# Input rows of the feed-forward part transposed on VectorE instead of TensorE, in a gated cross-attention block on one core

## The reference

```python
x = x + tanh(g_xattn) * xattn(layernorm(x), ctx)          # x: 2 x 2048 x 512, fp32
x = x + tanh(g_ffn)   * ffn(layernorm(x))
# ffn, w_gate and w_up (1536 x 512) and w_down (512 x 1536) int32, scaled by 1/127:
#   silu(x @ w_gate.T) * (x @ w_up.T) @ w_down.T
# xattn: 16 heads of 32, 77 context rows per batch, softmax over them, causal mask, output projection
```

## Time and profile before

| | |
|---|---|
| median of 3 runs | 874.59 us (873.66 to 875.28) |
| the profiled execution's own time | 874.07 us |
| its span, first to last instruction | 872.3 us |
| TensorE busy | 855.0 us (98%) |
| VectorE busy | 652.8 us (75%) |
| ScalarE busy | 460.5 us (53%) |
| GpSimd busy | 402.3 us (46%) |
| granted TensorE clock | 1.000 of full speed |
| FFN, four pairs | from 372.55 us to the end |

### The profile page before, as it was taken

How to read it: one execution, slowest core, us unless ns; L and a number is a source line. 1 busy time by engine, 2 the same in 40 slices (tenths; PEclk the granted TensorE clock), 3 DMA queues, 4 the chain that set the end, 5 groups by cost and what they waited for, 6 DMA issues and landing times.

```text
span 872.3 us, 12869 instructions
## 1 busy us (share of the span) xinstructions
PE 855.0 (98%) x4087; PEld 707.9 (81%) x4087; DVE 652.8 (75%) x1081; ACT 460.5 (53%) x1130; POOL 402.3 (46%) x344
## 2 busy tenths in 40 slices
PE   8999999999999999999999999999999999999997
PEld 7678888888888887788888888888888888888876
DVE  5988877778786877679688478788487877587882
ACT  5687575666666757446056264165362364460550
POOL 4665555556564664437144444155253255251350
PEclk9999999999999999999999999999999999999999
DMA  9233847272728131567333256043265143243302
GB/s 334 73 109 118 276 152 248 84 240 93 233 97 277 68 113 51 198 235 265 115 123 133 96 190 249 12 165 121 79 248 182 47 164 113 96 166 116 97 31 98
DMA packets 60406, 128.73 MB, mean 148 GB/s; under 512 B 7616, under 2 KB 20416, under 8 KB 60352
## 3 DMA queue, kind: packets, MB, share of 16 engines
q1 hardware_dynamic: 58960, 125.95, 41.7%
q10 hardware_dynamic: 1392, 2.10, 0.7%
HBM read 99.93 MB, written 27.79 MB: 146 GB/s over the span
## 4 chain that ended last, share of the span: by engine, by line
PE 87%; DVE 6%; ACT 3%; issue 1%; DMA 1%; POOL 1%; ACTq 0%; DVEq 0%
PE psum L1814 34%; PE psum L1548 29%; PE psum L1864 18%; PE psum L1573 4%; DMA gates<-g_ffn 1%; PE psum L1657 1%; ACT e L791 1%; POOL hT L696 1%; DVE bn L1034 1%; DVE e L1076 1%; DVE K L1128 1%; DVE mx L1073 1%; DVE qT L1058 0%; DVE pT L1047 0%; DVE aT L1058 0%
## 5 line engine op out<-in xcount | busy, mean ns | idle before, releaser
L1814 PE MATMUL psum<-xv,ring 128*128 128x512 f32 x1344 | 308.2, 390 | 0.9 <-ACT a L964 0.7
L1814 PEld LDWEIGHTS psum<-xv,ring 128*128 128x128 f32 x1344 | 251.5, 188 | 55.1 <-ACT a L964 1.1
L696 POOL TENSOR_TENSOR hT<-th,hT 128x512 fp32r<-128x512 f32 x48 | 86.3, 1798 | 201.2 <-ACT hT L984 201.2
L1864 PE MATMUL psum<-w_d,hT 128*128 128x512 f32 x768 | 177.7, 391 | 1.3 <-POOL hT L696 0.8
L1864 PEld LDWEIGHTS psum<-w_d,hT 128*128 128x128 f32 x768 | 143.7, 188 | 32.6 <-POOL hT L696 2.0
L554 POOL TENSOR_TENSOR e<-e,rden 128x616 f32<-128x616 f32 x64 | 77.9, 1217 | 110.4 <-DVE rden L1110 73.8
L791 ACT ACTIVATE e<-psum,nmx,q_scale 128x77 f32<-128x77 f32 x256 | 102.6, 427 | 2.3 <-DVE nmx L1090 2.2
L952 ACT ACTIVATE a<-psum 128x512 f32<-128x512 f32 x48 | 28.7, 599 | 131.7 <-PE psum L1814 131.4
L1428 DVE SCALAR_TENSOR_TENSOR acc<-psum,gate_ffn,acc 128x512 f32<-128x512 f32 x64 | 47.7, 750 | 65.1 <-PE psum L1864 65.1
L1548 PE MATMUL psum<-wo,aT 128*128 128x512 f32 x384 | 95.2, 399 | 0.5 <-DVE aT L1058 0.5
L1548 PE MATMUL psum<-xT,wq 128*128 128x512 f32 x360 | 89.0, 398 | 0.4 <-DVE qT L1058 0.4
(11 more groups left out here) (110 smaller groups left out, 1204.6 us busy)
## 6 DMA issues: line engine op xcount, KB each, us to landing
ring<-w_var SPq DMA_DIRECT2D x48, 896.0 KB, 4.6
w_var<-stage SPq DMA_DIRECT2D x12, 896.0 KB, 4.6
x_ln<-x SPq DMA_DIRECT2D x32, 256.0 KB, 4.6
x_res<-x SPq DMA_DIRECT2D x32, 256.0 KB, 5.0
x_mid<-x_res SPq DMA_DIRECT2D x32, 256.0 KB, 2.0
x<-x_mid SPq DMA_DIRECT2D x16, 512.0 KB, 5.6
acc<-x_mid SPq DMA_DIRECT2D x16, 512.0 KB, 6.4
out<-acc SPq DMA_DIRECT2D x32, 256.0 KB, 2.0
```

The costliest lines, as they stand in the source:

```text
L696: nc.gpsimd.tensor_tensor(hT[:, 1, i % HH, j, :], h[:, :], hT[:, 0, i % HH, j, :].bitcast(f32), ALU.subtract).then_inc(h_lo, 1)
L1814: last = nc.tensor.matmul(psum[:, bank, :], stat, mov, start=start and j == 0, stop=j == len(terms) - 1, skip_group_check=not start)
L1864: last = nc.tensor.matmul(m_bank[t % 2][:, :], hT[:, a, m, t // TT, (t % TT) * P:(t % TT + 1) * P], w_d[:, HH * h + m, :], start=m == 0 an ...
```

## The change

For pairs 1 to 3 (pair 0 stays as it is):

- The 32 TensorE transposes per pair are replaced by 32 VectorE transposes per pair, each of 32 partitions by 512 elements (`turn_rows`). They write `x2_t0` and `x2_t1` in SBUF. They are put at the end of slices 5 and 6 (two each), between the results of the first half's down tiles (two or three after each, 20 in all), and at the end of slices 7, 8 and 9 (three, three, two).
- The statistics move to slices 1 to 4. The normalisation moves from VectorE to GpSimd, in slices 3 and 4, after `h_low`.
- The load of the next pair's rows is issued at the start of the pair, all four DMAs in a row; for pair 1 before the last stores of attention.
- SiLU is one activation on ScalarE; both multiplies on VectorE go. The constant in `gate_ffn` follows.
- T1 and T3 are formed in slices 10 and 11 on VectorE, from SBUF, and written over the rows in `x2`, which are dead by then. T2 and T4 follow after slice 11. GpSimd's low part of T1 comes before its `h_low` of slice 11.
- The maximum over the gate and up weights is taken in all slices of the last pair, no longer in the first six of pair 0.
- At the end of a pair TensorE's order is rewritten: three down tiles are begun instead of two, the third in a bank of the slices, and their first slots are put before, between and behind p4 and p3.

```diff
+            def turn_rows(q, half_of, ops):
+                tiles = slice(TT * half_of, TT * half_of + TT)
+                dve.wait_ge(x2_normed, PT * q + TT * (half_of + 1))
+                if q > 1:
+                    dve.wait_ge(xb_lo, nth(XB_ORDER, q - 1, B22))
+                for op in ops:
+                    a, c = divmod(op, HG)
+                    rows = x2[a * HD:(a + 1) * HD, tiles, :].rearrange("p t (k n) -> p t k n", n=P)
+                    to = x2_t[half_of][c * HD:(c + 1) * HD].rearrange("p k (t n) -> p t k n", n=P)
+                    nc.vector.transpose(to[:, :, :, a * HD:(a + 1) * HD], rows[:, :, :, c * HD:(c + 1) * HD])\
+                        .then_inc(x2_turned, 1)
...
-                nc.scalar.activation(th1[:, :], psum[:, set_a[i % 2], :], ACT.Tanh, scale=0.5 * W_SCALE)\
-                    .then_inc(tanh1_done, 1)
+                nc.scalar.activation(th1[:, :], psum[:, set_a[i % 2], :], ACT.Silu, scale=W_SCALE)\
+                    .then_inc(silu1_done, 1)
...
                 if more:
-                    xv_copy(p + 1, B11, b11_at)
-                tanh2(last)
-                tanh1(last)
+                    xv_round(p + 1, B11)
+                silu2(last)
+                silu1(last)
                 if more:
-                    b12_copy(p + 1)
+                    xv_high(p + 1, T1)
                 h_high(last, 0)
+                if more:
+                    xv_round(p + 1, B21)
                 h_high(last, 1)
                 if more:
-                    xv_high(p + 1, T1)
-                    xv_copy(p + 1, B21, b21_at)
                     xv_high(p + 1, T2)
                     xv_high(p + 1, T3)
                     xv_high(p + 1, T4)
-                    b22_copy(p + 1)
+                    xv_round(p + 1, B22)
...
             def pair(p):
+                if 0 < p < NP - 1:
+                    sp.wait_ge(xv_lo, nth(LO_ORDER, p, T4))
+                    for j in range(TT):
+                        load_x2(p + 1, j)
                 for m in range(MH):
...
-                    if p + 1 < NP and m < TT:
-                        sp.wait_ge(xb_full, nth(TURNED, p, B21))
-                        load_x2(p + 1, m)
...
# GpSimd, in slice m behind h_low
-                    if p + 1 < NP and m == HH - 1:
-                        rstd_ahead(2 * p + 2)
-                        rstd_ahead(2 * p + 3)
+                    if p + 1 < NP and m in (2, 4):
+                        rstd_ahead(2 * p + 1 + m // 2)
+                        mean_ahead(2 * p + 1 + m // 2)
+                    if p + 1 < NP and m in (3, 4):
+                        normalise(2 * p - 1 + m)
+                    if p + 1 < NP and m == MH - 2:
+                        xv_low(p + 1, T1, T1)
...
# VectorE
+            FILL = (4, 6, 8, 11, 13, 16, 18, 21, 24)
             def first_half(p, more):
                 for t in range(PT):
-                    if more:
-                        stats2(2 * p + 2 + t // TT, t % TT)
...
                     result(p, 0, t)
-                    if more and t >= PT - 2:
-                        normalise2(2 * p + 2, range(2 * (t - PT + 2), 2 * (t - PT + 2) + 2))
-                if more:
-                    normalise2(2 * p + 3)
+                    if more:
+                        turns(p + 1, range(FILL[t], FILL[t + 1]))
...
# TensorE, end of a pair
-                if more:
-                    turn(p + 1, B11)
-                    turn(p + 1, B12)
+                early, late = range(HH - 2), range(HH - 2, HH - 1)
+                down(p, 1, 0, early)
                 p4(last)
+                down(p, 1, 1, early)
                 p3(last)
-                down(p, 1, 0, range(HH - 1))
-                down(p, 1, 1, range(HH - 1))
+                down(p, 1, 2, early)
+                for t in range(3):
+                    down(p, 1, t, late)
...
-                down(p, 1, 0, range(HH - 1, HH))
-                down(p, 1, 1, range(HH - 1, HH))
-                if more:
-                    turn(p + 1, B22)
-                    turn(p + 1, B21)
-                for t in range(2, PT):
+                for t in range(3):
+                    down(p, 1, t, range(HH - 1, HH))
+                for t in range(3, PT):
                     down(p, 1, t)
```

More of the change, by code:

```diff
@@ L1250, in form @@
+            def form(q, j):
+                if q:
+                    dve.wait_ge(x2_turned, turned(1, q))
+                else:
+                    if j == T1:
+                        dve.wait_ge(b12_kept, 1)
+                    dve.wait_ge(xb_full, nth(TURNED, 0, {T1: B11, T2: B22, T3: B22, T4: B21}[j]))
+                if j == T2:
+                    dve.wait_ge(v_formed, formed(q, T1))
+                if j == T4:
+                    dve.wait_ge(v_formed, formed(q, T2))
                 if j == T1:
-                    dve.wait_ge(b12_kept, q + 1)
@@ L1266, in xv_low @@
+                nc.vector.tensor_tensor(variant(q, j), one, other, ALU.subtract).then_inc(v_formed, 1)
             def xv_low(q, j, bank):
                 dve.wait_ge(xv_hi, nth(HI_ORDER, q, j))
-                nc.vector.tensor_tensor(xv[:, j, 1], pair_of(bank), xv[:, j, 0].bitcast(f32), ALU.subtract)\
+                full = {B11: b11, B21: b21, B22: b22}[j] if q else pair_of(bank)
+                nc.vector.tensor_tensor(xv[:, j, 1], full, xv[:, j, 0].bitcast(f32), ALU.subtract)\
                     .then_inc(xb_lo, 1)
@@ L1449, in widest, with turns @@
                 nc.vector.tensor_copy(wide[:, :], wide_f[:, :]).then_inc(wide_ready, 1)
+            def turns(q, ops):
+                for half_of in range(2):
+                    inside = [op - TURNS * half_of for op in ops if op // TURNS == half_of]
+                    if inside:
+                        turn_rows(q, half_of, inside)
+            FILL = (4, 6, 8, 11, 13, 16, 18, 21, 24)
             def first_half(p, more):
                 for t in range(PT):
-                    if more:
-                        stats2(2 * p + 2 + t // TT, t % TT)
-                    elif t < HH:
+                    if not more and t < HH:
                         dve.wait_ge(rd_used, HH)
@@ L1478, in pair @@
                         hidden2(i - 1)
-                    if p == 0 and m < HH or p == NP - 1 and m >= HH:
+                    if p == NP - 1:
                         largest_gu(i)
+                    if more and 1 <= m <= TT:
+                        for t in (2 * m - 2, 2 * m - 1):
+                            stats2(2 * p + 2 + t // TT, t % TT)
+                    if more and m in (HH - 1, HH):
+                        turns(p + 1, range(2 * (m - HH + 1), 2 * (m - HH + 2)))
+                    if more and HH < m < HH + 4:
+                        at = (24, 27, 30, 32)[m - HH - 1:m - HH + 1]
+                        turns(p + 1, range(at[0], at[1]))
+                    if more and m == MH - 2:
+                        form(p + 1, T1)
+                    if more and m == MH - 1:
+                        form(p + 1, T3)
                 gate2(last)
-                silu2(last)
                 if more:
                     xv_low(p + 1, B11, b11_at)
-                silu1(last)
                 hidden1(last)
@@ L1488, in pair @@
                 hidden2(last)
-                if not more:
+                if more:
+                    form(p + 1, T2)
+                else:
                     widest()
-                if more:
-                    form(p + 1, T1)
                 result(p, 1, 0)
                 result(p, 1, 1)
-                if more:
-                    form(p + 1, T2)
-                    form(p + 1, T3)
                 result(p, 1, 2)
@@ L1500, in pair @@
                     xv_low(p + 1, B21, b21_at)
-                    form(p + 1, T4)
                 result(p, 1, 3)
                 if more:
+                    form(p + 1, T4)
+                result(p, 1, 4)
+                if more:
                     xv_low(p + 1, B22, b22_at)
-                for t in range(4, PT):
+                for t in range(5, PT):
                     result(p, 1, t)
```

225 lines of the change are left out of this document (104 added, 121 removed).

## The result

The change made the kernel slightly slower. It takes 875.65 us (median of 12 runs, 875.37 to 877.38) against 873.88 for the kernel before (12 runs, 873.13 to 875.28): a ratio of 1.0021, interval 1.0013 to 1.003. The forecast was 866.5. The profiled execution took 875.89 us with a span of 874.0, and 874.07 with 872.3 before.

What follows compares the result with a forecast made beforehand. TensorE, busy 98% of the span, was taken to bound the kernel. Gains of 6.9 us (2.3 at each of three pairs' ends) and 1.2 (last pair) sum to 8.1, giving 866.5 us against the median; range 864 to 869.5, chance 0.65.

Steps and rivals of the forecast that it cites:

- the term 0.228 us a matmul: TensorE: time per matmul, read from 72 matmuls at a pair's end and used throughout the sum.
- nothing: GpSimd, slices 3 and 4: loads of 6.2 and 7.6 us against 6.4 cost TensorE no time; pair 0 up to half a microsecond.
- VectorE's transposes: VectorE: 0.68 us each, 22 us a pair for 32, covered by removed work; no cost to TensorE in the slices.
- The rival of a slow transpose: VectorE transposes at 1.21 us each stall TensorE 5.7 us a pair, 17 in all, giving 883.5 us; chance 0.08.
- SiLU: ScalarE: one extra table load before the first SiLU, `snap2` 0.25 us later, no cost; by the skill's figure 0.6 us worse.
- The rival of a load in each slice: ScalarE reloads its table at every change between SiLU and Copy: 53 us over 44 slices, near 920 us; chance 0.03.
- The end of a pair: TensorE at a pair's end: 3.9 us removed less 1.6 of new stalls, gaining 2.3 a pair, 6.9 for three.
- the zero of the forecast: At a pair's end: the point at which TensorE has issued p7 of slice 11, from which the steps are timed.
- the stall of 0.6: At a pair's end: TensorE waits for GpSimd's last `h_low`, ending at 9.2 us; 0.6 us, between 0 and 1.2.
- The wait for the result of tile 1: At a pair's end: TensorE's fourth down tile waits until tile 1's result is out; 0.8 us.
- The last pair: TensorE's end of the last pair: 2.2 us of gaps and 0.1 of transpose go, 0.9 of wait stays; gain 1.2 us.
- the rival of longer waits: Slow contended passes lengthen waits at pairs' ends and in slices, 12 us in all: about 873.5, no change; chance 0.04.

Runs made afterwards that it cites:

- b_moved: Kernel before, operations unchanged, with its SBUF buffers moved to the places they have in the kernel after: 880.92 us, ratio 1.0081.
- a_ring128: Kernel after with 128 unused bytes a partition ahead of `ring`, making its distance from `xv` a multiple of 256: 871.28 us, ratio 0.9973.
- a_ring256: Kernel after with 256 unused bytes a partition ahead of `ring`: 876.23 us (single run).
- a_norm5: Kernel after with GpSimd's second normalisation moved from slice 4 to behind `h_low` of slice 5: 871.19 us, ratio 0.9971.
- b_silu: Kernel before with SiLU as one ScalarE activation and both VectorE multiplies removed: 872.0 us, ratio 0.998.
- b_hid128: Kernel before with `region_b` 128 bytes longer, which moves `hT`/`pT` and `w_d` together: 875.18 us (single run).
- a_best: Kernel after with both operand distances 0 modulo 256, second normalisation one slice later, fourth down tile's own bank, last transposes 2, 3, 3: 860.93 us, ratio 0.9853.
- the comparison: The kernel before, unchanged, measured on the same chip as each follow-up kernel: 873.44 to 873.86 us.

## Why the forecast was wrong, step by step

**The sum: the term 0.228 us a matmul.** It was read from a stretch of down matmuls and taken over for all matmuls after the change without being put in doubt. The operands of that stretch, `hT` and `w_d`, kept their distance (49,152 bytes) through the change, and it kept its rate (227.1 and 227.6 ns). For the slices it was 0.2270 before and 0.2327 after: 5.7 ns more, 28 x 5.7 ns = 0.16 a slice, 7.7 us over 48 slices. This is the largest miss. That the placement is the cause is shown from both sides (`b_moved`, `a_ring128`, `a_ring256`), and that it is the distance, by the two groups together. The change had it in its lines on `causal`, `gap2` and `x2_t1`, which the forecast never priced.

**GpSimd: "nothing".** The loads of 6.2 and 7.6 us for slices 3 and 4 were near enough, though the normalising pass took 0.86 to 1.02 us and not the 0.77 of the earlier trace rows. The list of who waits was incomplete. It named ScalarE's SiLU and `upper2`; a third is the first down tile, which wants slice 5's `h_low` ten matmuls after it began. GpSimd's timeline in the second pair:

```profile
539.76 3.45 POOL L702 TENSOR_SCALAR x<-x,nmean,rstd 128x512 f32<-128x512 f32 x4
543.18 1.26 POOL L724 TENSOR_TENSOR hT<-th,hT 128x512 fp32r<-128x512 f32 x1
```

The normalisation ends at 543.18, the low part at 544.44, and TensorE goes on at 544.49. That is 1.5 us in each of three pairs, 4.5 in all, and `a_norm5` gave 4.5 back.

**VectorE's transposes: right.** 702 ns each against 0.68, and 2.17 us for three. None of TensorE's waits in the slices names VectorE. The rival of a slow transpose is out. The cover was thin, though: with the old matmul rate the group of 3 and 3 became visible (0.3 us a pair).

**SiLU: right.** One second table load:

```profile
378.87 1.28 ACT L1018 ACT_TABLE_LOAD   x1
380.16 0.63 ACT L1018 ACTIVATE th<-c 128x512 f32<-128x512 f32 x1
380.70 0.58 ACT L1011 ACTIVATE th<-psum 128x512 f32<-128x512 f32 x1
381.18 0.59 ACT L999 ACTIVATE a<-psum 128x512 f32<-128x512 f32 x1
```

The SiLU starts where the load ends, and `snap2` starts at 381.18, where 380.97 is its time before: 0.2 us late, as forecast. The 2.66 us of the Trainium skill ("ScalarE: Activation LUTs", What ACT_TABLE_LOAD costs) for such a switch do not show here; the measurement decides. (By that figure, and with 0.8 us to spare, the forecast's 0.6 should have been 0.25 + 1.38 - 0.8 = 0.8.) The rival of a load in each slice is out. That SiLU by itself is worth 1.8 us (`b_silu`) had not been counted apart.

**The end of a pair.** The low part of T1 starts 4.58 us after the zero of the forecast (596.92), takes 2.42, and `h_low` ends at 8.7 instead of 9.2. TensorE wants it at about that time, so the stall of 0.6 didn't come.

```profile
601.50 2.42 POOL L688 TENSOR_TENSOR xv<-x,xv 128x1024 fp32r<-128x1024 f32 x1 [1.85 <-ACT xv L961]
603.89 1.74 POOL L724 TENSOR_TENSOR hT<-th,hT 128x512 fp32r<-128x512 f32 x1
```

The wait for the result of tile 1 came, 0.73 to 0.75 us as listed and 1.09 from start to start, against 0.8. Taken together 1.1 for 1.6: three pairs are 1.5 us better than forecast, mostly because VectorE did not slow the low part of T1: it took 2.42 us, where 2.41 and a further 0.3 were put down for it.

**The last pair.** Its window is 0.25 us shorter, where 1.2 were forecast and 1.9 of slower slices belong to it, so its own part was 2.2, 1.0 better. About 0.85 of that lies behind the last matmul, between it and the end of the span: 5.24 us before and 4.38 after. That part is luck. The same stretch takes 4.73 us in `b_hid128`, which has the instructions of the kernel before, and 5.58 in `a_best`, which has the change; no run shows what sets it. Without it the forecast for the last pair was right to 0.2 us.

**The account.** 7.7 + 4.5 - 1.5 - 1.0 = 9.7 us, against 9.9 between forecast (-8.1) and measurement (+1.8). The measured time is close to the 873.5 of the rival of longer waits, but by other means: its slow `h_low` at the pair's end and its waits in the slices did not come. What the forecast said of the transposes, the SiLU and the wait for tile 1's result was right, and its wait for `h_low` at a pair's end was too pessimistic. Two steps failed: one rate for all matmuls, and nothing for GpSimd's later `h_low`. No run undoes these two alone; with the buffers placed, the normalisation moved, and also the bank added and the transposes spread, the kernel is 12.5 us below the comparison (`a_best`).

## What to carry to other kernels

A diff that adds, removes or resizes an SBUF buffer moves all that lie behind it. Work out the places of each matmul's two operands before and after, and when untouched matmuls change their mean duration, pad one buffer before looking for contention. Before costing late work at nothing, list everyone who waits for the engine's next product, those in the next stage too.

## What the runs showed of the hardware

With `xv` and `ring` at equal places modulo 256 bytes a slice matmul (128x128 by 128x512) starts each 227.0 ns; 64, 128 and 192 bytes off it is 229.2, 232.7 and 233.4 ns, and the same order shows in `pT` against `V`. The granted clock is 1.00 throughout. It holds from the first slice to the last, the last pair included, where the other engines have less to do. At 128 bytes the extra comes in one of two patterns in the intervals between starts: seven matmuls (228, 230, 232 and 241 ns among them, mean 232.4) or two by turns (229 and 238, mean 233.5). The kernel after changes from the first to the second and back between slices, so a short stretch does not give the mean. What in the chip makes it, and why the two signs differ, stays open. Only these two groups of matmuls were seen at several distances, and both have 512 columns. Distance 0 is not all that counts: attention's `xT` against `wq` and `wo` against `aT`, at distance 0 in every kernel, start each 229.2 to 229.9 ns.
